# A fill of 416 half-precision numbers behind each row scatter of two convolution stages

## The reference, cut to what matters

```
x = x + conv0(norm(x))   # router takes 2 of 4 experts per image: 3x3 convs, group norm, silu
x = x + ffn0(norm(x))    # per token: 2 of 8 gated experts, hidden 341
x = x + conv1(norm(x))   # per image: 9 tap weights from the pooled image, depthwise 3x3
x = x + ffn1(norm(x))    # per token: 1 of 8 experts, hidden 512, capacity 1.25 x share
```

## Time and profile before

| | |
|---|---|
| median of 3 runs | 2088.11 us |
| lowest and highest | 2087.66 and 2089.25 us |
| span of the profiled execution | 2373.5 us |
| profiled span minus median | 285.4 us |
| stage A, about | 100 to 990 us of the span |
| stage B, about | 990 to 1500 us |
| stage C, about | 1500 to 1960 us |
| stages D and F, about | 1960 to 2373.5 us |
| POOL busy | 1040.3 us (44%) |
| scatters of line 618 | 384, mean 1010 ns |

### The profile page before, as it was taken

How to read it: one execution, slowest core, us unless ns; L and a number is a source line. 1 busy time by engine, 2 the same in 40 slices (tenths; PEclk the granted TensorE clock), 3 DMA queues, 4 the chain that set the end, 5 groups by cost and what they waited for, 6 DMA issues and landing times.

```text
span 2373.5 us, 40208 instructions
## 1 busy us (share of the span) xinstructions
PE 1745.3 (74%) x8924; PEld 941.9 (40%) x8925; DVE 1521.7 (64%) x5423; ACT 1020.1 (43%) x1718; POOL 1040.3 (44%) x1196
## 2 busy tenths in 40 slices
PE   0387777776667775699999999287877868899822
PEld 0333333333333432354445445154544444444312
DVE  1856555545455554577777777476766647788678
ACT  0433333333233332476666667135455524555411
POOL 0003333333333334576566666525455344666600
PEclk9889888878888887799999999599899979999955
DMA  9300001001000002322222221412211013222044
GB/s 267 102 19 28 28 28 36 28 31 33 33 31 28 27 19 59 87 81 74 71 73 79 74 72 46 106 40 60 72 56 45 18 40 95 72 81 72 19 133 151
DMA packets 180085, 149.22 MB, mean 63 GB/s; under 512 B 19302, under 2 KB 161822, under 8 KB 179960
## 3 DMA queue, kind: packets, MB, share of 16 engines
q1 hardware_dynamic: 153336, 98.05, 14.9%
q0 software_dynamic: 26624, 49.93, 6.2%
HBM read 76.00 MB, written 77.34 MB: 65 GB/s over the span
## 4 chain that ended last, share of the span: by engine, by line
PE 38%; DVE 22%; issue 13%; another core or an unknown queue 11%; ACT 7%; POOL 5%; SPq 2%; DMA 1%; ACTq 1%; DVEq 1%; POOLq 0%
PE banks L734 10%; PE banks L736 9%; PE banks L735 9%; PE banks L729 6%; ACT work L1043 3%; POOL slot_rows L618 2%; SPq L429 2%; DVE small L1896 1%; PE banks L747 1%; PE banks L946 1%; DVE small L1392 1%; DVE small L1247 1%; POOL tokens L673 1%; POOL tokens L670 1%
## 5 line engine op out<-in xcount | busy, mean ns | idle before, releaser
L639 POOL DMA_INDIRECT ffn_rows<-work x448 | 471.0, 1051 | 293.9 <-issue 182.1
L618 POOL DMA_INDIRECT slot_rows<-work,small x384 | 387.8, 1010 | 325.5 <-issue 153.3
L729 PE MATMUL banks<-small,work 128*128 128x128 f32 x1472 | 239.9, 308 | 300.8 <-ACT work L1043 118.2
L729 PEld LDWEIGHTS banks<-small,work 128*128 128x128 f32 x1472 | 193.9, 158 | 379.4 <-issue 170.7
L1784 DVE TENSOR_TENSOR work<-work 128x512 f16<-128x512 f32 x376 | 261.4, 695 | 12.8
L734 PE MATMUL banks<-work,wb_h 128*128 128x512 f16 x648 | 247.7, 382 | 26.6 <-DVE work L1800 9.7
L735 PE MATMUL banks<-work,wb_h 128*128 128x512 f16 x648 | 247.0, 381 | 0.0
L736 PE MATMUL banks<-work,wb_l 128*128 128x512 f16 x648 | 246.9, 381 | 0.0
L734 PE MATMUL banks<-work,wa_h 128*128 128x512 f16 x576 | 243.4, 423 | 3.6 <-ACT work L1074 3.3
L735 PE MATMUL banks<-work,wa_h 128*128 128x512 f16 x576 | 243.1, 422 | 0.0
L736 PE MATMUL banks<-work,wa_l 128*128 128x512 f16 x576 | 241.9, 420 | 0.0
(11 more groups left out here) (307 smaller groups left out, 3110.6 us busy)
## 6 DMA issues: line engine op xcount, KB each, us to landing
wa_l<-slot_rows SPq DMA_DIRECT2D x112, 264.0 KB
work<-ffn_rows SPq DMA_DIRECT2D x48, 512.0 KB, 5.2
ffn_rows<-small SPq DMA_DIRECT2D x32, 256.0 KB, 3.7
work<-in_x SPq DMA_DIRECT2D x16, 512.0 KB, 3.3
out_image<-work SPq DMA_DIRECT2D x16, 512.0 KB, 2.6
ffn_rows<-work POOLq DMA_INDIRECT x448
slot_rows<-work,small POOLq DMA_INDIRECT x384
slot_rows<-small SPq DMA_DIRECT2D x17, 264.0 KB, 4.1
```

Of the source, the lines that this page charges most:

```text
L618: pool_e.indirect_dma_start(slots, bass.IndirectOffsetOnAxis(ap=slot_i[:, row_buffer(p, i, k), tt:tt + 1], axis=0), rows[row_buffer(p, i, ...
L639: pool_e.indirect_dma_start(dst, bass.IndirectOffsetOnAxis(ap=idg[old.v][:, qq, 0:1].bitcast(I32), axis=0), yt[old.u][:, qq, :], None, bou ...
L729: last = pe.transpose(dst[:, tt * P:(tt + 1) * P], x, ident)
```

## The change

A scratch buffer `breath` of 416 half-precision numbers per partition is cut from the end of the work area, and POOL fills it with zeros after each scatter. A fill waits for the fill before it, since they write the same place. Nothing reads the buffer.

```diff
         acc = [tA([PIX]) for _ in range(2)]
+        breath = tA([416], F16)
...
                         ).then_inc(sem(f"{p}scattered_rows{row_buffer(p, i, k)}"), 16)
+                        spaced = (i.b * choices + k) * TPI + tt
+                        if some(spaced):
+                            pool_e.wait_ge(sem(p + "spaced"), spaced)
+                            apart(pool_e)
+                        pool_e.memset(breath, 0.0).then_inc(sem(p + "spaced"), 1)
```

## The result

The changed kernel takes 2131.74 us in the median of four runs (2125.27 to 2136.37); the kernel before took 2088.68 beside it. The ratio is 1.0204, with an interval of 1.0189 to 1.0220: 43 us slower. The sign was as forecast and the time lies in the range of 2098 to 2232, but the forecast of 2175 had twice the loss (87 us).

The account below looks back on a forecast made before the run. Stage A was bound by PE, with the landing of `rows[0]` as next limit, stage C by a loop through POOL and DVE. 46.7 + 35.6 + 6 + 2 = 90 us on 2088 gave 2178, taken as 2175; range 2098 to 2232.

Parts of the forecast that it names:

- The price of a fill: On POOL between two scatters: each fill of 416 numbers costs 0.445 us, its whole length, with the idle 0.30 us kept.
- The ends of the range: Price per fill of 0.145 us if it covers the idle 0.30 (2116), or 0.63 with a round trip (2214).
- the two loops: Repeated losses: stage A's landing of `rows[0]`, 15 x 3.1 = 46.7 us; stage C's additions, ten times 3.56, 35.6 us.
- Nothing covers it, if `rows[0]` is late already: Stage A: seven fills land `rows[0]` 3.1 us later, all of it passed on to ACT and PE; 46.7 us.
- I cost both at nothing: Stage A, POOL's addition of line 653 and the copy to `rows[1]`: later but covered, 0; without cover up to 4 us a step.
- Stage C is a loop through POOL and DVE; the whole group of scatters lies on the chain: Stage C: nothing idle between additions 25.53 us apart; eight fills add 3.56 us, ten times, 35.6 us.
- the stall: Stage A, ACT's line 1100 waiting for "remote", 132.2 us in 13 steps; taken as mostly absent from timed runs.
- the 210 worked out: Stage A: fourteen steps, each 15 us shorter without the stall, make 210 of the recording's 285 us excess.
- The ends of the stages: Late scatters behind stage A delay the loads of B, 6 us; half the fills behind stage C, 2 us.
- Only C pays: Rival: in stage A the rows are wanted later than they land, so only stage C loses; 2129 us, chance 0.22.
- The faster case: Rival: timed runs stall at line 1100 in A too, and gaps between scatters let PE's signals out; 2073 us, chance 0.08.
- the growing stall: Rival: timed runs stall too and gaps don't end it; each burst of A grows 7.1 us; 2238 us, chance 0.08.

Follow-up runs that it names:

- a_first8: Kernel before plus fills of 416 numbers only behind the first eight scatters (those of `rows[0]`) of each image in stage A: 2118.06 us, ratio 1.0144.
- a_second8: Kernel before plus fills of 416 numbers only behind the second eight scatters (those of `rows[1]`) of each image in stage A: 2088.14 us, ratio 1.0001.
- a_half: Kernel before plus fills of 208 numbers instead of 416, in stage A alone: 2091.49 us, ratio 1.0016.
- after: The recording of the changed kernel, with all fills of 416 numbers in stages A and C; it spans 2126.4 us, against 2086.5 for the kernel before recorded again.

## Why the prediction was wrong

**The price of a fill.** Taken as 0.445 us, for want of a reason that a scatter's preparation starts under a fill. It was 0.32: the idle time fell from 0.30 to 0.17 us. The ends of the range (0.145 and 0.63) held it. With 0.32 the prediction's own sum would have been 33.6 + 25.6 for the two loops, and about 65 in all.

**Stage A.** The place was right: seven fills ahead of the landing of `rows[0]`, ACT's line 1043 behind it, PE behind that; a_first8 and a_second8 show that it is those fills alone. 15 x 7 x 0.32 makes 33.6, and 31.7 was measured, but a_half shows that this agreement is partly luck. Fifteen times seven times the 0.14 us of half a fill would make 15, and 3.3 was measured. "Nothing covers it, if `rows[0]` is late already" was too strong, and its condition held in only 10 of 15 steps. Some four tenths of the later landing were covered; the clock then took back part of the waiting with half fills and added a third of the loss with full ones. "I cost both at nothing", of the other eight scatters and of the addition behind them, was right.

**Stage C: the step that failed.** "Stage C is a loop through POOL and DVE; the whole group of scatters lies on the chain", 35.6 us; 9.8 was measured. In after the additions are 20.9 us apart where 29.1 was foretold:

```profile
1514.53 2.36 POOL L679 TENSOR_TENSOR tokens<-tokens,work 128x1024 f32 x1 [0.18 <-POOL tokens L676]
...
1535.47 2.36 POOL L679 TENSOR_TENSOR tokens<-tokens,work 128x1024 f32 x1 [0.18 <-POOL tokens L676]
```

In the kernel before, recorded again, a step of C takes 20.7 us, and POOL stands idle 1.6 to 2.5 us behind the additions. The chain of two of its steps (1401 to 1443 us) runs through PE, ACT and DVE and holds no instruction of POOL; PE's lines 946, 729 and 956 are 54% of it. The chain of the earlier trace rows came from the recording with the stall, and the stall stands in that chain's own steps. In that recording DVE's line 1921, which stands ahead of the statistics, waits for "remote" in 13 steps of C, 85.9 us in all, and starts each time 1.3 to 1.6 us behind the eighth scatter. First the step of the earlier trace rows, then a step of the kernel recorded again:

```profile
1659.94 0.23 DVE L1921 TENSOR_TENSOR small<-banks,small 128x64 f32<-128x64 f32 x1 [6.58 <-remote]
```

```profile
1412.14 0.23 DVE L1921 TENSOR_TENSOR small<-banks,small 128x64 f32<-128x64 f32 x1 [2.48 <-PE banks L956]
```

In the second it waits for PE alone and starts with two of the eight scatters still to come. So in that recording it was the stall that put the whole group of scatters on the loop of C. The prediction set it aside in stage A and read stage C as if it were sound.

**The stall.** That the timed runs don't have it was right; the kernel before has none when it is recorded again. Stage A held less of the 285 us than the 210 worked out: its last scatter ends 184 us earlier in the second recording. Stage C held some 5 us in each step, which the prediction didn't see. The Trainium skill (NOTIFIC — the notification-queue block, sections 6.4 and 7.1) lets the path of trace records hold back what writes to it. The runs neither show nor exclude that for the one recording: fourteen later ones hold no such wait.

**The ends of the stages.** 6 and 2 us. In after the last scatter of A ends 11.1 us later than the twelve steps explain, and 4.7 of it comes back before C. That leaves 6.4, where 6 were forecast beside three more landings of 3.1 each. Behind the fifteenth border copy of C after loses only 0.2 more.

**The rivals.** "Only C pays" gave 2129, near the measured 2132, for the wrong reason: A paid three quarters. The faster case and the growing stall fall with the stall.

## What to carry to other kernels

An operation put into an engine's queue costs what it adds between its neighbours, not its own length, and only ahead of the instruction that another engine waits for: here seven of sixteen fills in each burst of stage A. A loss should not be scaled from one size to another: in stage A a fill of half the length cost a tenth, since waiting was partly covered and the granted clock, higher with the one and lower with the other, decided the rest. Where a recorded execution is far longer than the timed ones, none of its stages is a sound basis, not only the one where the stall was found first: record it again, or look for the same kind of wait in each stage before reading it.

## What the runs showed of the hardware

- An indirect DMA on POOL had 0.30 us of idle time ahead of it behind another indirect DMA, 0.17 behind a fill of 416 or 208 numbers, and 0.19 behind one of 2. Fills of 0.12 us between two of them left these 1.28 us apart.
- Fills on POOL took 123 ns for 2 half-precision numbers, about 290 for 208, and 465 for 416.
- A two-input operation on DVE of 0.2 us took 2.38 us beside a two-input addition on POOL; one-input scaling of half-precision numbers on DVE went from 290 to 473 ns beside POOL's fills.
- The same 126 matmuls of a step of C took 18.99 us at a granted clock of 1.00 and 23.59 at 0.80, with 0.2 us more waiting of PE in the step; a step with 0.27 us more kept 1.00.
- One recording of the kernel before was 285 us longer than its runs, with waits for "remote" at ACT's line 1100 and DVE's line 1921 that ended 1.3 to 2.4 us behind POOL's bursts of scatters; a second one had none.
